# One graph-transformer kernel: source rows of the second attention moved into the edge turns, its score terms folded into the weights, all projections behind the edges

## The reference, cut to what matters

```python
h_e = jnp.einsum('nf,hfd->hnd', x, W_e)          # x: 625x512, 8 heads of 64
h_r = jnp.einsum('nf,hfd->hnd', x, W_r)
s_src = jnp.einsum('hnd,hd->hn', h_e, a_src)[:, src]
s_dst = jnp.einsum('hnd,hd->hn', h_e, a_dst)[:, dst]
diff = h_r[:, dst] - h_r[:, src]
score = s_src + s_dst + (diff . a_dif) + (|diff| . a_abs) + ((hr_src * hr_dst) . a_prd)
alpha = leaky_relu(score, 0.2)                   # softmax over the edges of one src
out = segment_sum(att * h_e[:, dst], src)
```

## Time and profile before

| | before |
|---|---|
| median of 3 runs | 1088.94 us (1088.46 to 1090.07) |
| the profiled execution | 1090.06 us, span 1088.2 us |
| PE busy | 982.1 us, 90% |
| DVE busy | 764.0 us, 70% |
| POOL busy | 347.5 us, 32% |
| mean granted TensorE clock | 0.959 |
| product `hre`, PE | from 613.37 us, 34.96 us |
| first gather issued | 656.94 us |
| last scatter issued | 877.22 us |

### The profile page before, as it was taken

The page is one execution under the profiler, slowest core; times in us unless marked ns, Lnnn a source line. Parts: engine busy times, 40 slices in busy tenths (PEclk is TensorE's granted clock), DMA queues, the critical chain, the costliest instruction groups (busy, mean ns, idle before and its releaser), DMA issues.

```text
span 1088.2 us, 12200 instructions
## 1 busy us (share of the span) xinstructions
PE 982.1 (90%) x4284; PEld 648.8 (60%) x4284; DVE 764.0 (70%) x1320; ACT 336.0 (31%) x613; POOL 347.5 (32%) x316
## 2 busy tenths in 40 slices
PE   7899999999899989999896988999887859988988
PEld 6874686544574447544463436776565528877864
DVE  8897697333795667744435468998987759999743
ACT  5873472312402231122114111321113303444511
POOL 1007720000301102001100116777777714555500
PEclk9999999999999999999898998999988976999999
DMA  9999210203300222001130325333333377541101
GB/s 306 294 306 274 64 79 1 85 12 115 126 1 1 91 59 90 1 0 56 48 115 1 134 48 155 99 99 98 98 93 95 89 284 292 207 163 40 63 1 47
DMA packets 66036, 115.10 MB, mean 106 GB/s; under 512 B 11473, under 2 KB 43473, under 8 KB 64445
## 3 DMA queue, kind: packets, MB, share of 16 engines
q1 hardware_dynamic: 57021, 93.08, 25.3%
q0 software_dynamic: 8960, 21.31, 7.1%
HBM read 85.88 MB, written 28.49 MB: 105 GB/s over the span
## 4 chain that ended last, share of the span: by engine, by line
PE 43%; DVE 27%; POOL 14%; issue 8%; DMA 7%; ACT 1%; SPq 0%; POOLq 0%; DVEq 0%; ACTq 0%
PE ps L748 17%; PE ps L886 7%; POOL arena L680 7%; DMA pairs<-arena,pairi 5%; PE ps L757 5%; DVE arena L1589 5%; POOL pairs L690 4%; PE ps L791 3%; PE ps L740 3%; DVE arena L1945 3%; DVE arena L1930 2%; PE ps L940 2%; DVE arena L1954 2%; PE ps L1093 2%; POOL small L639 1%
## 5 line engine op out<-in xcount | busy, mean ns | idle before, releaser
L748 PE MATMUL ps<-arena 128*125 128x512 f32 x400 | 179.7, 605 | 0.8 <-DVE xn L1623 0.8
L616 POOL TENSOR_TENSOR small<-small 125x1 f32<-125x1 f32 x50 | 34.9, 698 | 390.4 <-DVE small L1402 390.4
L748 PE MATMUL ps<-arena,xnT 128*125 128x512 f32 x280 | 125.7, 607 | 5.0 <-DVE x L1856 4.2
L748 PEld LDWEIGHTS ps<-arena 128*125 128x125 f32 x400 | 75.5, 193 | 90.2 <-issue 89.2
L973 PE MATMUL ps<-ex_low,high 125*125 125x512 f32 x400 | 107.3, 416 | 0.0
L1248 ACT ACTIVATE arena<-ps,cols 128x125 f32<-128x125 f32 x120 | 43.2, 466 | 202.9 <-PE ps L740 202.9
L748 PEld LDWEIGHTS ps<-arena,xnT 128*125 128x125 f32 x280 | 53.5, 193 | 70.4 <-issue 69.0
L690 POOL DMA_INDIRECT pairs<-arena,pairi x80 | 86.9, 1086 | 25.5 <-issue 25.5
L740 PE MATMUL ps<-ident,arena 125*125 125x125 f32 (+3 forms) x425 | 63.0, 285 | 26.5 <-ACT arena L1105 8.8
L973 PEld LDWEIGHTS ps<-ex_low,high 125*125 125x125 f32 x400 | 74.6, 195 | 16.7 <-issue 0.5
L740 PEld LDWEIGHTS ps<-ident,arena 125*125 125x125 f32 (+3 forms) x425 | 54.4, 170 | 48.8 <-issue 17.3
(11 more groups left out here) (215 smaller groups left out, 1811.6 us busy)
## 6 DMA issues: line engine op xcount, KB each, us to landing
pairs<-fill SPq DMA_DIRECT2D x10, 2500.0 KB, 21.9
arena<-in_mw SPq DMA_DIRECT2D x6, 2048.0 KB, 8.4
arena<-pairs SPq DMA_DIRECT2D x4, 2500.0 KB, 13.9
arena<-pairs SPq DMA_DIRECT2D x8, 1250.0 KB, 6.0
arena<-pairs SPq DMA_DIRECT2D x8, 625.0 KB, 6.4
arena<-in_rows SPq DMA_DIRECT2D x16, 250.0 KB
arena<-in_qkv_w SPq DMA_DIRECT2D x1, 3072.0 KB
arena<-in_cw SPq DMA_DIRECT2D x3, 1024.0 KB, 5.3
```

Of the source, the lines that this page charges most:

```text
L748: last = mm(slot[0:m, lo:hi], lhsT_of(k), rhs_of(k)[:, lo:hi], start=(k == 0), stop=(k == ks - 1))
```

## The change

The product `hre` is split. Ahead of the edges only `hr` (512 columns, from W_r) is computed for each tile. The `h_e` half becomes five pieces of beside-work named `he`: one ahead of turn 0 and one each in turns 0, 2, 4 and 6. Each consists of 4 x 2 large matmuls and 4 x 2 small ones with 16 columns, whose weights `terms` are the attention vectors folded into W_e and W_r: DVE forms them from `wer`, `fold_destinations` between the layer norms of the tiles and `fold_sources` after the first one-hots. ACT empties `he` with two copies. POOL no longer waits for `tmp_free`. The steps of the second mixing stand in later turns, the last three row turns and all five projections behind turn 39. SP loads `wo1` only when the last `he` is emptied.

```diff
-KEYS = (1, 3, 5, 7)
-QUERIES = (9, 11, 13, 15)
-VALUES = (16, 18, 19, 21, 23)
-KEYS_TURNED = (24, 25, 26, 27)
-CONTEXT = 29
-ATTENDED = (30, 31, 32, 33)
-ROWS_TURNED = (32, 33, 34, 35, 36, 37, 38, 39)
-PROJECTED = (34, 36, 38, TURNS, TURNS + 1)
+HE = (-1, 0, 2, 4, 6)
+KEYS = (7, 9, 11, 13)
+QUERIES = (14, 16, 18, 19)
+VALUES = (21, 23, 24, 26, 28)
+KEYS_TURNED = (29, 30, 31, 32)
+CONTEXT = 34
+ATTENDED = (35, 36, 37, 38)
+ROWS_TURNED = (35, 36, 37, 38, 39, TURNS, TURNS + 1, TURNS + 2)
+PROJECTED = (TURNS, TURNS + 1, TURNS + 2, TURNS + 3, TURNS + 4)
...
+            ring.wait_emptied(sp, ("he", NT - 1))
             load(wo1, w("w_outT"), "wo1_loaded")
...
-            pool.wait_ge(sig("tmp_free"), 1)
...
-                slot = ring.claim(pe, ("hre", i))
+                slot = ring.claim(pe, ("hr", i))
                 ring.wait_emptied(pe, ("xnT", 2, i))
-                ring.filled(product(slot, P, nodes(xnT, i), lambda k: wer[:, k, :], KC, 2 * D))
+                ring.filled(product(slot, P, nodes(xnT, i), lambda k: wer[:, k, D:2 * D], KC, D))
...
+            def sources(i):                      # PE
+                slot = ring.claim(pe, ("he", i))
+                for k in range(KC):
+                    mm(slot[0:P, 0:D], xnT[:, k, P * i:P * (i + 1)], wer[:, k, 0:D],
+                       start=(k == 0), stop=(k == KC - 1))
+                    last = mm(slot[0:P, D:D + 2 * H], xnT[:, k, P * i:P * (i + 1)],
+                              terms[:, k].rearrange("p n h -> p (n h)"),
+                              start=(k == 0), stop=(k == KC - 1))
+                ring.filled(last)
...
-            ring.wait_emptied(pe, ("hre", NT - 1))
-            pe.wait_ge(sig("hrx_ready"), NT)
+            ring.wait_emptied(pe, ("hr", NT - 1))
             edge_turn(0)
+            pe.wait_ge(sig("terms_ready"), KC)
+            sources(0)
...
+            def fold_destinations(k):            # DVE
+                st.did(TT(folds[:, 0, :], wer[:, k, 0:D], a_ends[:, 1, :], ALU.mult))
+                st.wait()
+                v.tensor_reduce(terms[:, k, 0, :], by_head(folds[:, 0, :]), AX_X, ALU.add)\
+                    .then_inc(sig("folded"), 1)
+                v.wait_ge(sig("folded"), k + 1)
+            def fold_sources(k):
+                st.did(TT(folds[:, 1, :], wer[:, k, 0:D], a_ends[:, 0, :], ALU.mult))
+                st.did(TT(folds[:, 2, :], wer[:, k, D:2 * D], a_ends[:, 2, :], ALU.mult))
+                st.wait()
+                st.did(TT(folds[:, 1, :], folds[:, 1, :], folds[:, 2, :], ALU.subtract))
+                st.wait()
+                v.tensor_reduce(terms[:, k, 1, :], by_head(folds[:, 1, :]), AX_X, ALU.add)\
+                    .then_inc(sig("terms_ready"), 1)
...
                 if i:
                     normed_x(i - 1)
+                    fold_destinations(i - 1)
             normed_x(NT - 1)
...
             one_hots_of_edges(0)
             one_hots_of_edges(1)
+            for k in range(KC):
+                fold_sources(k)
```

More of the change, by code:

```diff
@@ L124, in psum_jobs @@
                    lambda i: [], lambda i: [(("xnT", 2, i), "act")])
-    jobs += [(("hre", i), "dve") for i in range(NT)]
+    jobs += [(("hr", i), "act") for i in range(NT)] + [(("he", 0), "act")]
     for e in range(PROJECTED[-1] + 1):
-        for turns, name, who in ((KEYS, "kT", "act"), (QUERIES, "qT", "act"),
+        for turns, name, who in ((HE, "he", "act"), (KEYS, "kT", "act"), (QUERIES, "qT", "act"),
                                  (VALUES, "v1", "dve"), (KEYS_TURNED, "kn", "act"),
@@ L371, in build_gps @@
         wer = view(5000, KC, 2 * D)
-        ar = view(9096, 4, D, parts=P)
+        a_abs = view(9096, D)
+        a_ends = view(24100, 3, D)
+        folds = view(0, 3, D)
+        terms = small[:, 128:192].rearrange("p (k n h) -> p k n h", k=KC, n=2)
         hea = view(11144, NT * H * (HD + 1) + WIDE - HD - 1, parts=P)
@@ L532, in _ @@
             load(wer, w("w_er"), "gat_loaded")
-            for n, name in enumerate(("a_abs", "a_src", "a_dst", "a_dif")):
-                load(ar[:, n, :], row(name), "gat_loaded")
+            load(a_abs, row("a_abs", 128), "gat_loaded")
+            for n, name in enumerate(("a_src", "a_dst", "a_dif")):
+                load(a_ends[:, n, :], row(name, 128), "gat_loaded")
             ring.wait_emptied(sp, ("f0o", NT - 1))
@@ L1024, in _ @@
                     edge_product(e)
+                if e in HE:
+                    sources(HE.index(e))
                 if e in KEYS:
@@ L1038, in _ @@
                     h = ROWS_TURNED.index(e)
+                    ring.wait_emptied(pe, ("he", NT - 1))
                     turn(("rT", h), lambda k: hrx[:, k, h, :], [HX] * NT, lambda k: 128 * k)
@@ L1278, in _ @@
             for i in range(NT):
-                slot = ring.wait_filled(act, ("hre", i))
+                slot = ring.wait_filled(act, ("hr", i))
                 act.activation(hrx[:, i, :, 0:HD],
-                               slot[0:P, D:2 * D].rearrange("p (h e) -> p h e", h=H), ACT.Copy)\
+                               slot[0:P, 0:D].rearrange("p (h e) -> p h e", h=H), ACT.Copy)\
                    .then_inc(sig("hr_copied"), 1)
-                act.activation(hr_high[:, i, :], slot[0:P, D:2 * D], ACT.Copy)\
-                   .then_inc(sig("hr_high_ready"), 1)
+                ring.emptied(act.activation(hr_high[:, i, :], slot[0:P, 0:D], ACT.Copy), ("hr", i))
             def edge_turned(e):
@@ L1293, in edge_turned, with sources @@
                    .then_inc(sig("hotsT_ready"), 1)
+            hea4 = hea[:, 0:NT * H * (HD + 1)].rearrange("p (i h e) -> p i h e", i=NT, h=H)
+            def sources(i):
+                if i == 0:
+                    act.wait_ge(sig("hea_ready"), 2)
+                slot = ring.wait_filled(act, ("he", i))
+                act.activation(hea4[:, i, :, 0:HD],
+                               slot[0:P, 0:D].rearrange("p (h e) -> p h e", h=H), ACT.Copy)
+                ring.emptied(act.activation(
+                    hrx[:, i, :, HD:HX],
+                    slot[0:P, D:D + 2 * H].rearrange("p (n h) -> p h n", n=2), ACT.Copy), ("he", i))
             def kq_turned(name, dst, bias, j):
@@ L1325, in rows_turned @@
                                             bias=prdx_of(1, h)), ("rT", h))
-            for e in range(TURNS + 1):
+            for e in range(ROWS_TURNED[-1] + 2):
                 if e < TURNS:
                     edge_turned(e)
+                if e - 1 in HE:
+                    sources(HE.index(e - 1))
                 if e - 1 in KEYS:
```

50 lines of the change are left out of this document (14 added, 36 removed).

## The result

| | before | after |
|---|---|---|
| median of the runs | 1088.70 us (1087.45 to 1090.07, 4 runs) | 1075.49 us (1074.21 to 1077.35, 4 runs) |
| ratio | | 0.988, 95% interval 0.986 to 0.990 |
| profiled execution, span | 1090.06 us, 1088.2 us | 1074.21 us, 1072.4 us |

The change makes the kernel 13 us faster; 1073 was forecast, inside 1065 to 1081. The same kernel in a later set of six runs took 1078.96 us, ratio 0.9907 (0.9892 to 0.9921), so its gain lies between 0.8 and 1.4%.

A forecast was written before the change was run, and what follows sets the result against it. The prediction took POOL's queue, started by the first gather, to set the edge stage's pace. Entry -21.2 us and work behind the edges +5.1 gave -16.1, so 1073 us, range 1065 to 1081.

The forecast's parts named there:

- Bound: Edge stage: POOL's queue of DMA issues sets the pace, 5.54 us a turn, and the first gather is what matters.
- Entry, -21.2: Up to the first gather: half the product -17.5 us, the fold +0.8, the wait behind ACT's last copy -4.5.
- the fold between the norms: `fold_destinations(3)` on DVE between the last two layer norms: +0.8 us, bounds 0 and 1.4.
- the tail: In the entry: ACT's last copy to first gather, 3.5 us for 8.0, -4.5. In the sum: work behind the edges, +5.1.
- Cover of the folds, 3 us: Ahead of turn 0: DVE ends its folds near 630, some 3 us before PE can begin `sources(0)` near 632.8.
- Turns 0 to 8: First edge turns: an `he` piece takes 4.4 us, leads are 3 and 2 us, POOL stays the pace, cost 0.
- The pace, 0 with 4 either way: Edge turns: lengthened POOL issues beside DVE's L1866 stay as costly in sum; change 0, with 4 us either way.
- Loads, 0 to +1: `wo1` load in turn 7 beside scatters: a late landing does no harm; taken as 0, bound +1 us.
- Context: Context moved from turn 29 to 34: the scores of turn 39 still precede their scatter by 1.1 us.
- Behind the edges, +5.1: After turn 39: the chain of projections and additions through one slot delays the end of the merges by 5.1 us.
- the rival "more": Tail or turns cost more: lower PE clock 3 us, dear small records 3, unlucky meetings 4; 1079 us, chance 0.23.
- Sum: Whole kernel: entry -21.2 and the stretch behind the edges +5.1 give -16.1 us, so 1073 us.

The follow-up runs named there:

- after_again: The changed kernel once more, unchanged, measured in a later set of runs: 1078.96 us, ratio 0.9907 to the kernel before.
- he_ahead: The changed kernel with all five `he` pieces ahead of turn 0: 1090.69 us, ratio 1.0013 to the kernel before.
- one_hot_single: The changed kernel with a one-input compare in place of the two-input L1896, leaving the destination's half out of the product: 1073.93 us, ratio 0.9869 to before.

## Why the prediction was right, step by step

*Bound.* Right: with POOL's queue as the pace, 22 us less ahead of the first gather came out as 13 us less in all, and the ledger accounts for each part.

*Entry, -21.2.* Measured -22.0. The product gave -17.8 (-17.5 forecast), the fold between the norms +0.2 (+0.8; from the last `out_f0` to the first `hr` product it is 4.98 us in place of 4.78), the tail -4.4 (-4.5). Of this tail the sum was right and its parts were not: from ACT's copy to the landing it took 3.26 us where the output store had lent 2.7, and POOL started 0.31 us behind the landing and not 0.85. That the two cancel, 3.57 us against 3.5, is luck. A second thing was luck too: 17.18 us is the product at the higher clock throughout. Ten of the thirteen profiles of the new kernels show 19.2 us, and 28.8 us to the first gather where they show 26.4. The chain of waits of `after_again`:

```profile
609.69 1.09 PE ps L744 x4
610.79 19.15 PE ps L752 x40
```

From 610 to 620 us PE was granted 0.77 there and 1.00 in after; in the stretch ahead, 600 to 610, it had been busy for 7.2 of 10 us in both (granted 1.00 in after, 0.89 there). Of before's 34.96 us the same holds (0.83 in that window). The Trainium skill, TensorE: Matmul & The Clock Gate, Part 1, has throttled as the default state, which activity lifts; nothing here shows why like activity ends at either level. These 2.4 us are most of the spread that I see between profiles in this stage.

*Cover of the folds, 3 us.* It held with nothing to spare: DVE ended them at 629.78, PE began the piece at 629.84. Four of DVE's multiplications had taken 1.4 to 1.7 us and not 0.69, while POOL made `hr_low`. In `after_again`, with the slower product, the folds ended 3.4 us ahead of the piece.

*Turns 0 to 8.* Right: a piece 4.32 us (4.4), leads 3.57 and 2.42 us (3 and 2), POOL the pace, and PE at the higher clock in every window from 645 to 795 us. `he_ahead` shows what the leads were worth.

*The pace, 0 with 4 either way.* +1.1 us over 36 turns, +0.8 and +0.7 around them (the +0.8 because three of the first eight gathers were lengthened, to 1.29, 1.36 and 1.57 us, and in before one, to 1.57). The number held, in part by luck: the same turns took 198.4 to 205.2 us in other profiles, and 205.2 is beyond the 4 us that were allowed. Two readings of it did not hold. The turns were to be 15 us shorter with no issue beside L1866; with L1896 (its line in after) replaced they were 5.5 to 6.1 us shorter. And the prediction said that issues beside the subtraction stay mostly at 0.98 us. They do so only when they begin near its end; in before four of nine were above 1.1 us, and what they follow is in the last section. So the rule of the Trainium skill, GPSIMD Engine Reference, Specifications, was borne out for both instructions.

*Loads, 0 to +1.* The mechanism was wrong. It said that a late scatter does no harm, as it has 5.5 us to land. Half of the scatters of after land within 2.4 us, but the one issued at 671.44, beside the load, took 6.97 (7.62 in `after_again`), and POOL waited 2.30 us for it (2.91). How much of that was given back in the turns that follow is open.

*Context.* Right: the scores of turn 39 were 1.99 us ahead of their scatter (1.1 forecast), after 4.93, 3.92 and 2.56 in the three turns before.

*Behind the edges, +5.1.* Mis-sized by 1.4: measured +6.5. Addition 0 ended 0.9 us behind the last scatter and not 0.1, the next round of projection and addition took 5.34 us and not 4.9, the three after it 12.2 and not 11.9; the merges gave back 0.2. Of the rival "more", its 3 us for a lower clock did not come: PE had 1.00 from 845 to 870.

*Sum.* -16.1 forecast, -13.3 measured. The stages taken as 0 add 2.2 us (0.77 + 1.10 + 0.68 - 0.38), the tail 1.4, and the entry takes 0.8 back: 2.8 in all.

## What to carry to other kernels

Where one queue sets the pace, the event that starts it is what counts: work can go from ahead of it to between its turns for little, as long as the lead of the first turn lasts (13.8 of 17.3 us came back when it didn't). Cut profiles of two kernels at the same events: three edits to the tail saved 2.5 to 6.4 us where they were made, and in two of the profiles the turns ahead took most of it back, which no total would have shown. But see first how much a stage varies when its instructions don't change: here by 7 us. And before a second bottleneck is removed, look at the lead that the next engine has in each turn, not at its busy share: PE was at 29 to 30 of 30 us both where POOL was the pace and where it no longer was.

## What the runs showed of the hardware that was not expected

**An issue of POOL waits for the end of a DVE instruction; it isn't slowed.** In after, an issue that begins t us into a DVE instruction of L us with two inputs in SBUF, or into the one-input f16 compare L1893, takes L - t + 0.87 us (within 0.05), where that is above 0.98. Where both begin within 0.02 us of each other the issue stays at 0.96 to 0.99 (3 in after). L1896 at 0.11 of 0.87: 1.63; the subtraction L1928 at 0.36 of 0.69: 1.19; in `one_hot_single` the one-input f16 compare at 0.11 of 0.38: 1.14. Issues that begin beside the fp32 reduction (53 in after) or the rise that reads PSUM (16) stay at 0.98.

**And it goes both ways, which brings the two in step.** Of the 36 compares L1893 of after between 645 and 840 us, 17 begin 0.27 to 0.48 us ahead of the end of an issue; each ends 0.12 to 0.17 us behind it, at 0.43 to 0.61 us in place of 0.38. L1896 then starts 0.16 to 0.20 us behind the issue's end, and the next issue, due after POOL's 0.30, meets nearly its whole length (1.57 to 1.63 us, all 17). One such place in the timelines of after, DVE and then POOL:

```profile
712.71 0.48 DVE L1893 TENSOR_SCALAR arena<-arena 125x625 f16<-125x625 f16 x1
713.22 0.87 DVE L1896 SCALAR_TENSOR_TENSOR arena<-arena 125x625 f16<-125x625 f16 x1
```

```profile
712.06 1.00 POOL L695 DMA_INDIRECT pairs<-arena,pairi  x1 [0.30 <-issue]
713.37 1.58 POOL L685 DMA_INDIRECT arena<-table,srci  x1 [0.30 <-issue]
```

So these meetings are not left to chance, as "the same instructions meet with another offset" had it, and it may be why before and after have 32 and 31 long issues. It isn't all: 19 of the 36 compares had no such meeting, and other profiles with the same turns have 28 to 42 long issues. The Trainium skill, SBUF — State Buffer, "SBUF: two separate sides", calls the pair of ports that the two engines share an exclusive lock and not a split bandwidth; the rows agree. A reduction put between L1893 and L1896 might break the step; it wasn't tried.
